# Two pairs of part slots in turn, layer 0's norms by batch, routing sums on GpSimd, and one root on VectorE

## The reference

```python
x = x + tanh(g_xattn[0]) * cross_attention_0(layernorm(x), ctx, ctx)   # 16 heads of 16
x = x + tanh(g_ffn[0])   * experts(layernorm(x))                       # 8 experts, top 2
x = x + tanh(g_xattn[1]) * cross_attention_1(layernorm(x), ctx, ctx)   # with biases
x = x + tanh(g_ffn[1])   * quantised_gated_ffn(layernorm(x))
```

## Time and profile before

| | |
|---|---|
| median of 3 runs | 958.4 us (956.46 to 959.63) |
| the profiled execution | 958.25 us |
| its span, first to last instruction | 956.4 us |
| mean granted TensorE clock | 0.957 |
| layer 0: first score product of group 0 | 55.12 us |
| layer 1: first score product of group 0 | 533.22 us |
| layer 1: first product of the last feed-forward | 782.29 us |
| last down projection begins (L2077) | 909.23 us |

### The profile page before, as it was taken

How to read it: one execution, slowest core, us unless ns; L and a number is a source line. 1 busy time by engine, 2 the same in 40 slices (tenths; PEclk the granted TensorE clock), 3 DMA queues, 4 the chain that set the end, 5 groups by cost and what they waited for, 6 DMA issues and landing times. The chain is left out here.

```text
span 956.4 us, 13634 instructions
## 1 busy us (share of the span) xinstructions
PE 860.7 (90%) x4064; PEld 434.0 (45%) x4065; DVE 634.4 (66%) x1286; ACT 497.3 (52%) x659; POOL 154.4 (16%) x263
## 2 busy tenths in 40 slices
PE   6879999999986999999998799999999979993098
PEld 3532333333353666666665333333333554441087
DVE  5969888888771222222348888888887478688932
ACT  1426777777741111111114467777777684597650
POOL 1223011111164000000025133100004404000000
PEclk9999999999997999999999899999999989997589
DMA  8586856664455111110147793333320000000011
GB/s 250 173 219 141 211 123 168 167 166 134 134 176 171 34 33 33 33 32 28 33 134 233 205 241 82 77 81 78 79 58 2 1 1 0 1 0 0 0 39 50
DMA packets 71325, 91.38 MB, mean 96 GB/s; under 512 B 26086, under 2 KB 56934, under 8 KB 71270
## 3 DMA queue, kind: packets, MB, share of 16 engines
q1 hardware_dynamic: 63564, 67.96, 28.0%
q0 software_dynamic: 5584, 19.93, 6.2%
q10 hardware_dynamic: 2128, 2.89, 0.9%
HBM read 62.90 MB, written 27.44 MB: 94 GB/s over the span
## 5 line engine op out<-in xcount | busy, mean ns | idle before, releaser
L1337 DVE TENSOR_REDUCE MX<-PS 128x1 f32<-128x512 f32 x512 | 320.7, 682 | 44.0 <-PE PS L1796 43.0
L940 ACT ACTIVATE Pt<-PS 128x1024 f32<-128x1024 f32 x256 | 248.3, 1021 | 102.4 <-PE PS L1817 102.4
L1796 PE MATMUL PS<-KSt,BIG 96*128 96x512 bf16 x512 | 176.2, 388 | 14.7 <-DVE BIG L1253 10.4
L1817 PE MATMUL PS<-BIG,KSt 99*128 99x512 bf16 x512 | 151.0, 381 | 0.2 <-DMA BIG<-MR 0.2
L1828 PE MATMUL PS<-Pt,VS 128*17 128x512 f32 x1024 | 136.1, 598 | 0.0
L1796 PEld LDWEIGHTS PS<-KSt,BIG 96*128 96x128 bf16 x512 | 40.7, 97 | 160.3 <-DVE MX L1337 99.0
L1971 PE MATMUL PS<-BIG,KSt 128*128 x184 | 85.2, 607 | 0.7 <-DVE KSt L1463 0.4
L1993 PE MATMUL PS<-BIG,Pt 128*128 x368 | 84.2, 382 | 1.1 <-DVE Pt L1458 1.1
L1458 DVE COPY Pt<-PS 128x512 f32<-128x512 f32 x46 | 29.7, 686 | 81.8 <-PE PS L1982 81.8
L2059 PE MATMUL PS<-KSt,BIG 128*128 128x512 f32 x192 | 83.2, 593 | 0.7 <-ACT BIG L1042 0.7
L1817 PEld LDWEIGHTS PS<-BIG,KSt 99*128 99x128 bf16 x512 | 49.9, 98 | 53.4 <-ACT Pt L940 2.4
(11 more groups left out here) (199 smaller groups left out, 1029.9 us busy)
## 6 DMA issues: line engine op xcount, KB each, us to landing
qk_parts<-BIG SPq DMA_DIRECT2D x64, 192.0 KB, 3.1
BIG<-in_w POOLq DMA_DIRECT2D x12, 1024.0 KB, 5.9
BIG<-qk_parts SPq DMA_DIRECT2D x32, 192.0 KB, 3.3
KSt<-qk_parts SPq DMA_DIRECT2D x32, 192.0 KB, 3.8
v_rows<-BIG SPq DMA_DIRECT2D x8, 544.0 KB, 5.1
VS<-v_rows SPq DMA_DIRECT2D x32, 136.0 KB, 3.0
BIG<-qk_parts SPq DMA_DIRECT2D x32, 128.0 KB, 3.9
KSt<-qk_parts SPq DMA_DIRECT2D x32, 128.0 KB, 4.0
```

The costliest lines, as they stand in the source:

```text
L940: act.activation(PP[:, 2 * (kc % 2) + half, :, :].rearrange("p h t -> p (h t)"), ST[half], ACT.Exp, scale=DK ** -0.5).then_inc(exp_done, 1)
L1337: dve.tensor_reduce(MX[:, g % 2, i % TB, i // TB:i // TB + 1], ring(i), AX.X, ALU.max, negate=True).then_inc(max_taken, 1)
L1796: pe.matmul(ring(i), QS[0:ROWS, g, h, qc * P:(qc + 1) * P], KS[0:ROWS, g, h, :], start=True, stop=True).then_inc(max_done, 1)
L1817: last = pe.matmul(ST[half][:, i * S:(i + 1) * S], KS[0:ROWS + PARTS, g, h, kc * P:(kc + 1) * P], QS[0:ROWS + PARTS, g, h, :], start=True, ...
```

## The change

- `TURN` gives the blocks k0, q0, q1, q2 the first pair of part slots and k1, k2, k3, q3 the second, in turn. `landed` counts stores by it.
- SP stores the values of batch 2 before the loads of groups 0 and 1 instead of between them, and waits for one store instead of two before those loads.
- In layer 0 the norms are taken in three parts: batch 0, batch 1, batches 2 and 3. Their root is ScalarE's square root with the refinement on VectorE. VectorE's order in `prep_first` changes with it.
- The counting products on TensorE come after the values of batch 0. The sums over tiles and experts move from VectorE to GpSimd, into groups 0 and 3 of the first batch of attention; the division by 128 rounded up is done in floating point.
- In layer 1 the low parts of q0 move from VectorE to GpSimd, behind the gathers, and the rests of q1 move behind the root of the tiles `back`.
- In the tail of layer 1 the root of `ffn_a` is by Newton steps on VectorE, in two pieces around update 10. ScalarE loads the square root's table by a dummy operation after tile 12 and writes six of the ten normed tiles two at a time after the copies of tiles 13, 14 and 15.
- TensorE starts with 14 products of constants (28 instructions) whose result is not used.

```diff
         rt = [sb(f"rt{i}", [P, E]) for i in range(4)]
-        rti = [sb(f"rti{i}", [P, E], I32) for i in range(2)]
...
         placed = sem("placed")
+        tile_sums = sem("tile_sums")
...
+        TURN = {("k", 0): (0, 0), ("k", 1): (1, 0), ("q", 0): (0, 1), ("k", 2): (1, 1),
+                ("q", 1): (0, 2), ("k", 3): (1, 2), ("q", 2): (0, 3), ("q", 3): (1, 3)}
...
-            return c if kind == "k" or p == B - 1 else KC + c
+            return KC * TURN[kind, p][0] + c
...
-            return 32 * (((B + 1) * layer + (B if kind == "q" else p)) if slot(kind, p, 0) == 0 else (B - 1) * layer + p)
+            return 32 * (B * layer + TURN[kind, p][1])
...
-        NORMS = [("first0", range(2 * TB)), ("first1", range(2 * TB, NT)), *[(f"moe{h}", range(2 * h, 2 * h + 2)) for h in range(TB)], ("rest", range(ROUTED, NT)), ("back", range(ROUTED)),
+        NORMS = [("first0", range(TB)), ("first1", range(TB, 2 * TB)), ("first2", range(2 * TB, NT)), *[(f"moe{h}", range(2 * h, 2 * h + 2)) for h in range(TB)], ("rest", range(ROUTED, NT)), ("back", range(ROUTED)),
                  ("ffn_a", x_tiles(FFN_A)), ("ffn_b", x_tiles(FFN_B))]
-        NORM_NO = {"ffn_a": 0, "ffn_b": 1}
+        NORM_NO = {"first0": 0, "first1": 1, "first2": 2, "ffn_b": 3}
...
                 store_parts(layer, "k", 2)
+                store_values(layer, 2)
                 for c in range(KC):
-                    sp.wait_ge(part_out[slot("k", 0, c)], landed(layer, "k", 1))
...
                 load_stack(layer, 0, 0)
-                store_values(layer, 2)
...
             def attention(layer):
-                for c in range(KC):
-                    sp.wait_ge(part_out[c], 32 * (B + 1) * (layer + 1))
-                    sp.wait_ge(part_out[KC + c], 32 * (B - 1) * (layer + 1))
+                for j in range(2 * KC):
+                    sp.wait_ge(part_out[j], 32 * B * (layer + 1))
...
                         gather(i)
+                    low_parts(1, "q", 0)
...
+            def route_tiles():
+
+                steps = 0
+                gp.wait_ge(ranks_taken, 1)
+                gp.memset(before[:, 0, :], 0.0).then_inc(tile_sums, 1)
+                for i in range(1, ROUTED):
+                    steps += 1
+                    gp.wait_ge(tile_sums, steps)
+                    gp.tensor_tensor(before[:, i, :], before[:, i - 1, :], totals[:, i - 1, :], ALU.add).then_inc(tile_sums, 1)
+                gp.wait_ge(tile_sums, ROUTED)
+                gp.tensor_tensor(rt[0][:, :], before[:, ROUTED - 1, :], totals[:, ROUTED - 1, :], ALU.add).then_inc(tile_sums, 1)
+                gp.wait_ge(tile_sums, ROUTED + 1)
+                gp.tensor_scalar(rt[1][:, :], rt[0][:, :], 1.0 / P, (P - 1) / (2.0 * P), ALU.mult, ALU.add).then_inc(tile_sums, 1)
+                gp.wait_ge(tile_sums, ROUTED + 2)
+                gp.tensor_scalar(rt[1][:, :], rt[1][:, :], MAGIC, 1.0, ALU.add, ALU.mult).then_inc(tile_sums, 1)
+                gp.wait_ge(tile_sums, ROUTED + 3)
+                gp.tensor_scalar(rt[1][:, :], rt[1][:, :], -MAGIC, 1.0, ALU.add, ALU.mult).then_inc(tile_sums, 1)
+
+            def route_upto():
+
+                gp.wait_ge(tile_sums, ROUTED + 4)
+                gp.tensor_copy(upto[:, 0:1], rt[1][:, 0:1]).then_inc(tile_sums, 1)
+                for e in range(1, E):
+                    gp.wait_ge(tile_sums, ROUTED + 4 + e)
+                    gp.tensor_tensor(upto[:, e:e + 1], upto[:, e - 1:e], rt[1][:, e:e + 1], ALU.add).then_inc(tile_sums, 1)
...
                     load_w1(NG * (n - 1) + g)
+                elif g == 0:
+                    route_tiles()
+                elif g == 3:
+                    route_upto()
...
                     gp.wait_ge(ab_in, AB_IN[0])
-                    for c in range(KC):
-                        gp.wait_ge(part_out[c], 32 * (B + 1))
-                        gp.wait_ge(part_out[KC + c], 32 * (B - 1))
+                    for j in range(2 * KC):
+                        gp.wait_ge(part_out[j], 32 * B)
...
+                if layer == 0:
+                    norm("first0")
...
                 two_parts(layer, "k", 0)
+                if layer == 0:
+                    norm("first1")
...
                 if layer == 0:
+                    norm("first2")
...
+            def write_norm(some):
+
+                for i in some:
+                    t = x_tile(1, i)
+                    act.activation(XF[:, t, :], X[:, t, :], ACT.Identity, scale=rstd[:, i:i + 1],
+                                   bias=shift[:, i:i + 1]).then_inc(xf_act, 1)
...
                         copy_weight(0, i - W0_AT, 6 + (i - W0_AT) % 2)
-                    if layer and i == FFN_A[-1] + 3:
-                        norm("ffn_a")
+                    if layer and i >= NT - 3:
+                        act.wait_ge(ln_rstd, 1)
+                        write_norm(FFN_A[2 * (i - NT + 3):2 * (i - NT + 3) + 2])
+                    if layer and i == W0_AT + 2:
+                        act.activation(table[:, :], zrow[:, 0:1], ACT.Sqrt)
...
-            def write_norm(some):
...
-            act.wait_ge(ln_rstd, 1)
-            write_norm(FFN_A)
+            write_norm(FFN_A[6:])
...
-            def route_tiles():
-                dve.wait_ge(ranks_taken, 1)
-                link(dve, dve.memset(before[:, 0, :], 0.0))
-                for i in range(1, ROUTED):
-                    link(dve, dve.tensor_tensor(before[:, i, :], before[:, i - 1, :], totals[:, i - 1, :], ALU.add))
-                link(dve, dve.tensor_tensor(rt[0][:, :], before[:, ROUTED - 1, :], totals[:, ROUTED - 1, :], ALU.add))
-
-                link(dve, dve.tensor_scalar(rti[0][:, :], rt[0][:, :], float(P - 1), None, ALU.add))
-                link(dve, dve.tensor_scalar(rti[1][:, :], rti[0][:, :], 7, None, ALU.arith_shift_right))
-                link(dve, dve.tensor_copy(rt[1][:, :], rti[1][:, :]))
-                link(dve, dve.tensor_copy(upto[:, 0:1], rt[1][:, 0:1]))
-                for e in range(1, E):
-                    link(dve, dve.tensor_tensor(upto[:, e:e + 1], upto[:, e - 1:e], rt[1][:, e:e + 1], ALU.add))
             def route_places():
+                dve.wait_ge(tile_sums, ROUTED + 4 + E)
...
                 for i in tiles:
-                    if name in ("first0", "first1") and i % TB == 0:
+                    if name in ("first0", "first1", "first2") and i % TB == 0:
...
                 cols = norm_cols(name)
-                tiles = NORM_TILES[name]
-                for i in tiles:
+                for i in FFN_PARTS.get(name, NORM_TILES[name]):
...
                 link(dve, last)
-                link(dve, dve.tensor_scalar(ve[:, cols], mv[:, tiles[0]:tiles[-1] + 1, 1], EPS, None, ALU.add))
+                link(dve, dve.tensor_scalar(ve[:, cols], mv[:, cols, 1], EPS, None, ALU.add))
...
                 cols = norm_cols(name)
-                link(dve, norm_rstd(name))
...
                 rests(0, "k", 0)
-                root_norm("first0")
+                link(dve, norm_rstd("first0"))
+                norm_writes("first0", 0, 0, NORM_TILES["first0"])
                 take_values(0, 0)
-                norm_writes("first0", 0, 0, NORM_TILES["first0"])
+                route_ranks()
+                link(dve, norm_stats(NORM_TILES["first1"], "first1"))
+                norm_var("first1")
                 rests(0, "k", 1)
+                link(dve, norm_rstd("first1"))
                 take_values(0, 1)
-                link(dve, norm_stats(NORM_TILES["first1"], "first1"))
+                norm_writes("first1", 0, 1, NORM_TILES["first1"])
+                link(dve, norm_stats(NORM_TILES["first2"], "first2"))
+                norm_var("first2")
                 rests(0, "q", 0)
-                root_norm("first1")
                 rests(0, "k", 2)
+                link(dve, norm_rstd("first2"))
                 take_values(0, 2)
-                norm_writes("first1", 0, 2, NORM_TILES["first1"])
+                norm_writes("first2", 0, 2, NORM_TILES["first2"])
...
                 rests(1, "q", 0)
-                low_parts(1, "q", 0)
...
                 link(dve, norm_stats(NORM_TILES["back"], "back"))
-                rests(1, "q", 1)
...
                                          ALU.mult, ALU.mult).then_inc(back_shift, 1)
+                rests(1, "q", 1)
...
             route_slots()
-            route_ranks()
-            norm_stats(range(TB), "first0")
-            route_tiles()
-            link(dve, norm_stats(range(TB, 2 * TB), "first0"))
+            link(dve, norm_stats(NORM_TILES["first0"], "first0"))
+            norm_var("first0")
...
             link(dve, late_stats(range(8, 10)))
-            norm_var("ffn_a")
+            root_begin("ffn_a")
             update_late(10)
+            root_end("ffn_a")
+            norm_shift("ffn_a")
             update_late(11)
-            norm_shift("ffn_a")
...
             col_abs_max(0, 8, 6)
+            link(dve, norm_rstd("ffn_b"))
...
         def _(pe):
```

(15 more changed lines are left out.)

## The result

The changed kernel takes 948.56 us (median of 4 runs, 948.03 to 948.83), the kernel before 957.76 (4 runs, 956.46 to 959.63): ratio 0.9915, 95% interval 0.9897 to 0.9934. It is 9.2 us faster where 2.7 was forecast. Its profiled run took 948.79, its span is 946.9.

The account below looks back on a forecast made before the run. TensorE, busy 90%, was taken as the bound, with gains only from chains ahead of the first scores and the tail. Layer 0 -1.0, layer 1 -2.0, tail +0.3 from 958.25, plus 0.15, gave 955.7 us; range 951.9 to 959.8.

Parts of the forecast that it names:

- a start d earlier is an end d earlier: Attention from first score to end: TensorE nearly full, so gains at the start carry through unchanged: 1.0 and 2.0 us.
- The clock's recoveries: Half-clock spells after idles, 3.3 us at 55 and 6 at 533, fall differently: 1.3 us either way.
- Layer 0's start: Preparation before layer 0's attention: first score at 54.1 for 55.12, 1.0 us gained; between 0.3 lost and 2.7 gained.
- The table load: Layer 0, ScalarE: 1.28 us load after aggregation and epsilon at 13.3, so load and root end at 14.9.
- The contention: Layer 0: GpSimd's low parts (2.27 us) stretch VectorE's 1.0 us refinement, which ends 2.9 behind k0's rests.
- The stack loads: Layer 0, group 0: last of six issued at 49.8, lands 4.3 later at 54.1, the last wait before the first score.
- Layer 1's start: Preparation before layer 1's attention: first score at 531.2 for 533.22, 2.0 us gained; ends 1.0 and 3.1.
- A new spell: Sign of a wrong forecast: a half-clock run on TensorE appearing where none was before; no size given.
- The tail: Layer 1's tail, ten tiles' root on VectorE: project 11 about 1 us later, 0.3 lost overall (0.3 gained to 1.4 lost).
- Less contention: Only tensor_scalar waits for GpSimd: layer 0 gains 2.7, layer 1 3.1, tail loses 0.3; 952.9 us, chance 0.2.
- Given back: Freed slot fails: k1 waits for root in layer 0, gathers set q0's low parts in layer 1; 958.0 us, chance 0.15.
- Store ahead of the loads: Value store before group 0's stack loads delays them: layer 0's first score 4.0 late, layer 1 no gain; 962.6, chance 0.1.

Follow-up runs that it names:

- the slots alone: Kernel before with only the part slots used in turn (`TURN`, `slot`, `landed` and their waits): 962.66 us for 963.83, ratio 0.999.
- Old slots: Changed kernel with the part slots and waits of before: 954.73 us for the kernel before's 957.78, ratio 0.9968, on a quiet chip; 0.9983 on a restless one.
- old store: Changed kernel with the store of values 2 back behind group 0's stack loads: 954.44 us for the kernel before's 957.78, ratio 0.9964, quiet chip; 0.999, restless.
- the old tail: Changed kernel with the tail's `ffn_a` root back on ScalarE, all ten writes behind it: 950.05 us for the kernel before's 957.78, ratio 0.9914.
- fills in the kernel before: Kernel before with 20 small unused products in TensorE's idle ahead of both first scores: 953.35 us for 957.78, ratio 0.9949; first try, restless chip, 0.9963.
- holding the changed kernel's starts back: Changed kernel with both first scores waiting for small linked memsets on VectorE: 956.70 us, ratio 0.9998 to the kernel before; changed kernel beside it 950.10.
- more fills: Changed kernel with unused products: 13 ahead of first scores 950.39 us (0.9934); also ahead of experts and in last stage 951.01 (0.9933); unmodified 0.9926.

## Why the prediction was wrong

The forecast was 955.7, its range ended at 951.9, and 948.6 came.

- **The step that failed** is "From there to the end of the attention TensorE is nearly full, so a start d earlier is an end d earlier". The clock's recoveries, 3.3 and 6 us long behind the two scores, were only a margin of 1.3 us either way. The stretches behind the first scores became 5.3 us shorter, where the sum had nothing for them. The row for it stood in the trace before: the half clock near 509 was read as the price of an idle of 3.4 us, but for the idles of 5.5 and 5.0 ahead of the scores the same price wasn't charged. Nor was it asked what the change does to TensorE's idle ahead of q1's projection, where the new spells now fall (from 41.2 and 515.7).
- **Layer 0's start**, forecast 1.0, came at 1.9. The table load was put in the path. It ran at 5.54, under the wait for x; k0's rests ended 1.75 us earlier than forecast, and the chain behind kept that. The contention was sized right: with GpSimd's low parts beside them (15.34 to 17.61), the refinement's two products with both operands in SBUF took 1.14 and 1.08; in the tail of layer 1, with GpSimd idle, the same product over six columns took 0.17 (765.39). By the rule of the Trainium skill (page "SBUF — State Buffer", section "Who interferes with whom") a VectorE instruction with two SBUF inputs contends with a GpSimd instruction that reads SBUF. The trace agrees.
- **The stack loads** as the last wait of layer 0: right, and 0.9 earlier. Two errors meet in it: the last of the six was issued 1.85 earlier than forecast (47.95 for 49.8) and took 5.1 to land where 4.3 was taken.
- **Layer 1's start**: 2.2 for 2.0, with the named waits (value store, GpSimd's low parts, root without stretching). The half clock near 509 went, and came back at 515.7 under q1's projection, where it delays nothing. A new spell was named as a sign of being wrong; one came in each layer, and it shortened the idle ahead of the score without delaying the score.
- **The tail**: 0.3 lost was forecast, the profiles of the two tails differ by 0.9 up to the feed-forward and 0.4 to the end. Project 11 waits for update 10 as said.
- **The rivals.** Less contention: its mechanism is refuted by 1.14 and 1.08, and that its 952.9 is nearer is luck. Given back: the slots alone show no gain, but in the sum they are worth 4 to 5 us. Store ahead of the loads: the reverse, that line is worth 4 to 5 us.
- **Adding up the edits** is doubtful with it. Old slots or old store each give back more than half of the 7.7 us that the changed kernel with the old tail gained on that quiet chip, and the slots alone showed nothing. That fits a gain which hangs on where the spells fall; the intervals are too wide to show it.

Some 4 to 5 of the 9.2 us are the clock's, shown from two sides: fills in the kernel before gain 4.4 with no shorter chain, and holding the changed kernel's starts back by 2.1 us loses 6.6. What decides whether a given idle is followed by a spell, and why more fills bring nothing further, stays open.

## What to carry to other kernels

Ahead of a stage in which TensorE is the bound, read the idle before its first product and the granted clock behind it in the windows view, and charge the slower stretch to that idle: here edits that moved the two starts by 1.4 and 1.8 us were worth 4 to 5. Before shortening a chain for it, try a few idle products in the gap; here one line in the kernel before took half of the whole gain on a quiet chip. Look also at the idle before that one: a spell that falls on work nobody waits for is cheaper than one at the start of a full stage. And compare such edits in the full kernel, not only one at a time.

## What the hardware showed that I had not expected

- The changed kernel's ten runs on one restless chip went from 953.3 to 967.5 us, with mean granted clocks between 0.949 and 0.962; on a quiet chip its six went from 948.5 to 951.5, with 0.960 to 0.966. One profile tells such a kernel apart from another only by stretches, not by its span.
- ScalarE's table load ran ahead of the semaphore wait of the instruction that needs it: 1.28 us from 5.54, for a square root at 12.91, that cost nothing here.
- In three profiles of one restless chip (before with fills, old slots, old store) the transposes ahead of layer 1's queries gave their result late. In the profile of the kernel before with fills, TensorE's timeline and ScalarE's have:

```profile
506.45 1.04 PE L1734 MATMUL PS<-identf,OT 128*128 128x128 f32 x8
```

```profile
510.77 0.60 ACT L871 ACTIVATE BIG<-PS 128x512 f32<-128x512 f32 x1 [0.49 <-remote]
519.22 0.60 ACT L871 ACTIVATE BIG<-PS 128x512 f32<-128x512 f32 x1 [7.86 <-remote]
```

The copies wait for these transposes alone, which the profile has done at 507.5; the second copy starts at 519.22, and the way to layer 1's first score was 46.0 us for 36.9. In the changed kernel's first profile the same transposes stand at 499.54 and both copies are done at 501.3. The cause wasn't found.
